# TensorE's written order in two causal attentions: at a tie the second-pass step goes ahead of the first-pass job

## The reference, cut to what matters

```python
scores = jnp.einsum('bhqd,bhkd->bhqk', q, k) * scale
scores = jnp.where(causal, scores, -jnp.inf)
attn = jax.nn.softmax(scores, axis=-1)
out = jnp.einsum('bhqk,bhkd->bhqd', attn, v)
```

## Time and profile before

| what | us |
|---|---|
| median of 3 runs (range) | 2225.05 (2218.56 to 2233.74) |
| the profiled execution, device time | 2212.26 |
| its span | 2210.4 |
| PE busy in the span | 1749.5 (79%) |
| DVE busy | 1322.6 (60%) |
| ACT busy | 915.0 (41%) |
| a2a, first job to last DVE operation | 1208.1 to 1482.2 |
| a3a, X.1 of unit 0 to last DVE operation | 1711.9 to 1952.2 |

### The profile page before, as it was taken

One profiled execution on the slowest core, in us unless ns is written; L12 is line 12 of the kernel. 1 busy time (PEld: TensorE's weight loads), 2 busy tenths in 40 slices (PEclk: granted clock), 3 DMA queues, 4 the chain that ended last, 5 costly groups with the idle time before them and its releaser, 6 DMA issues. The chain is left out here.

```text
span 2210.4 us, 33923 instructions
## 1 busy us (share of the span) xinstructions
PE 1749.5 (79%) x12419; PEld 806.9 (37%) x12439; DVE 1322.6 (60%) x2669; ACT 915.0 (41%) x1719; POOL 408.8 (18%) x335
## 2 busy tenths in 40 slices
PE   5895999737888888888475798885984998859998
PEld 3633444313333433333232343433432344333333
DVE  3224444767557766674416788805465888437888
ACT  1110222325655656565342366651222566632221
POOL 0000000166456656563003000000001000000000
PEclk8797999858999999899887799987986899979999
DMA  4100000277566666664004211000005011000000
GB/s 131 47 17 1 0 0 0 68 193 183 137 147 170 158 165 146 165 155 103 11 7 132 53 27 31 17 1 1 0 20 175 16 31 31 2 1 0 0 0 19
DMA packets 193024, 141.40 MB, mean 64 GB/s; under 512 B 55865, under 2 KB 174825, under 8 KB 192746
## 3 DMA queue, kind: packets, MB, share of 16 engines
q1 hardware_dynamic: 186250, 127.35, 22.4%
q10 hardware_dynamic: 6624, 12.06, 1.9%
HBM read 78.75 MB, written 59.90 MB: 63 GB/s over the span
## 5 line engine op out<-in xcount | busy, mean ns | idle before, releaser
L1639 DVE TENSOR_REDUCE a1a_partial<-a1a_room 128x4 f32<-128x1024 f32 x192 | 226.0, 1220 | 52.5 <-PE a1a_room L1704 52.1
L1598 ACT ACTIVATE a1a_probsT<-a1a_st 128x512 f32<-128x512 f32 (+1 forms) x416 | 204.9, 580 | 55.4 <-PE a1a_st L1737 55.1
L2061 ACT ACTIVATE a3a_probsT<-a3a_st 128x512 f32<-128x512 f32 (+2 forms) x320 | 155.2, 562 | 112.7 <-PE a3a_st L2123 70.4
L2061 ACT ACTIVATE a2a_probsT<-a2a_st 128x512 f32<-128x512 f32 (+2 forms) x320 | 155.4, 561 | 109.7 <-PE a2a_st L2123 67.2
L1978 DVE TENSOR_REDUCE a3a_maxima<-a3a_room 128x2 f32<-128x1024 f32 (+3 forms) x160 | 170.1, 1112 | 35.3 <-PE a3a_room L2094 23.0
L1978 DVE TENSOR_REDUCE a2a_maxima<-a2a_room 128x2 f32<-128x1024 f32 (+3 forms) x160 | 170.2, 1112 | 29.0 <-PE a2a_room L2094 19.7
L745 DVE TENSOR_TENSOR f_mid<-f_b,f_act 128x512 f32<-128x512 f32 x96 | 66.3, 691 | 158.9 <-ACT f_act L707 158.9
L1774 PE MATMUL a1a_ctx<-a1a_probsT,a1a_vpad 128*9 128x512 f32 (+3 forms) x1408 | 151.2, 531 | 0.8
L1503 POOL TENSOR_TENSOR a1a_shifted<-a1a_shifted,a1a_best 128x1024 f32<-128x1024 f32 x64 | 121.6, 1901 | 144.2 <-DVE a1a_best L1645 144.0
L707 ACT ACTIVATE f_act<-f_a 128x512 f32<-128x512 f32 x100 | 59.7, 597 | 203.8 <-PE f_g L678 181.2
L1704 PE MATMUL a1a_room<-stack 48*128 48x128 bf16 (+1 forms) x1376 | 112.9, 265 | 28.8 <-DVE a1a_partial L1639 14.4
(11 more groups left out here) (477 smaller groups left out, 3407.8 us busy)
## 6 DMA issues: line engine op xcount, KB each, us to landing
a1a_bands<-a_band SPq DMA_DIRECT2D x112, 192.0 KB, 3.9
a_near<-a1a_shifted SPq DMA_DIRECT2D x112, 192.0 KB, 2.9
a1a_near<-a_near SPq DMA_DIRECT2D x64, 256.0 KB, 4.1
a_band<-a1a_r_mix SPq DMA_DIRECT2D x64, 254.0 KB, 3.7
stack<-q SPq DMA_DIRECT2D x96, 96.0 KB
stack<-k SPq DMA_DIRECT2D x32, 96.0 KB
q<-a1j_parts ACTq DMA_DIRECT2D x10, 256.0 KB, 3.1
q<-a_last_parts ACTq DMA_DIRECT2D x10, 256.0 KB, 4.2
```

What stands on the lines that cost most here:

```text
L1598: nc.scalar.activation(dst, src, ACT.Exp).then_inc(exp_done, 1)
L1639: nc.vector.tensor_reduce(partial[:, g % 2, :, 1 + r].rearrange("p (a s) -> p a s", a=2), src, X_AXIS, ALU.max).then_inc(job_free, 1)
L2061: nc.scalar.activation(probsT[:, block_at % BLOCK_ROOMS, place:place + heads, lo:], src, ACT.Exp).then_inc(exp_done, 1)
```

## The change

```diff
-            if max(now, event_at) < max(now, job_at):
+            if max(now, event_at) < max(now, job_at) + 1:
                 events.pop(0)
                 order.append(event)
```

## The result

The changed kernel takes 2269.70 us (median of 4 runs, 2266.04 to 2274.09) against 2229.39 (4 runs beside it, 2218.56 to 2234.05): a ratio of **1.0189, 95% interval 1.0143 to 1.0234**. It is slower, by 1.4 to 2.3%. Forecast were 2277 us, 2236 to 2302. The profiled execution took 2266.04 us (span 2264.2) against 2212.26, 53.8 more; 52 was forecast for that difference.

A forecast was written before the change was run, and what follows sets the result against it. DVE was taken to set the period first, with TensorE nearly full too. Per attention 1.2 + 7 x 34.2 + 26.0 = 266.6 us against 240.7; 52 us more for two, put on the 2225 median: 2277 us, range 2236 to 2302.

The forecast's parts named there:

- The tail: From turn X7.1 to DVE's last operation, only half 1 of unit 7 is left: 26.0 us, a gain of 20.8.
- X0.1 later: Turn X0.1 comes 1.2 us later, because products of unit 0 now go ahead of its last jobs.
- X.1 to X.0: Five jobs with nothing beside them, then an instruction run seen before, at half clock, in every unit: 12.3 us.
- X.0 to S: From turn X.0 to first step S: 7 products with steps, and 10 jobs mostly hidden beside them: 13.4 us.
- S to X.1: From first step S to turn X.1: 12 steps, 3 products, a context and 4 jobs, paced by TensorE and ACT: 8.5 us.
- The period: One unit of the attention, sum of its three stretches: 34.2 us against 27.7 before; break-even 30.5.
- The sum: Per attention 266.6 us against 240.7, 25.9 more; 52 us more for two attentions.
- the period is set by DVE first: In the old order's unit period, DVE sets the pace, with about 24.2 us of records in 27.7.
- the pace comes from steps that wait for a bank until ACT has read it: In X.0 to S, waits for ACT's reading set the pace, 2.56 us a product, with a 0.47 us wait seen.
- The full-clock rival: Clock stays full behind X.1 because waits there are short: period 32.1 us, total 2247; chance 0.20.
- shorter tail pays: Jobs fill all waits from S to X.1, clock full: period 30.3 us, total 2222, not slower; chance 0.12.
- Deeper spells: Half clock lasts past X.0 into the next product groups: period 36.0 us, total 2302; chance 0.11.

The follow-up runs named there:

- the added reductions: One more short DVE reduction ahead of every second job, on the changed order and the old order, both with clock-keeping matmuls: 2267.01 and 2233.45 us, one run each.
- with the clock held: Changed order plus matmuls of 128 columns filling waits at lone jobs, rows and tail context turns: 2244.65 us, ratio 1.0128 to the kernel before.
- the run from unit 5: Kernel before, with ties going to the step only from second-pass unit 5 on, plus the added matmuls filling waits: 2200.68 us, ratio 0.9923.
- the first experiment: Tie rule changed in attention a2a alone, a3a keeping the order of the kernel before: 2249.78 us, one run.

## Why the prediction was right

- **The tail** was forecast at 26.0 us and is 25.8. Its terms held: 0.6 us to the rows' DMA, 2.7 for the rows (2.9 forecast), 22.5 for half 1. The last was luck in part, since the clock was at half for 6.5 us of it, as it had been before for 6.4; with the same 28 steps behind X7.1 and nothing added there, five other tails took 32.0 to 32.7 us at half clock for the most part, which the forecast did not price.
- **X0.1 later** by 1.2: from the first job to X0.1 it is 34.67 us for 33.32 in a2a and 37.54 for 36.29 in a3a, so 1.35 and 1.25.
- **X.1 to X.0**: 12.3 forecast, 12.59 measured, as one spell of half clock in every unit. The spell lasts 10.2 us (1383.4 to 1393.6) in eleven of fourteen periods, not 13; TensorE was back at full speed as X.0 came, and so the stretches after it were undisturbed.
- **X.0 to S**: 13.4, measured 13.37. **S to X.1**: 8.5, measured 8.12. The period: 34.2, measured 34.08. The terms were off by +0.29, -0.03 and -0.38, which cancel; that is luck, on a small scale.
- **The sum**: 25.9 per attention was forecast, 27.2 and 24.7 came; with 1.9 us in the rest of the program 53.8 in all. On the medians it is 40, 12 less than forecast: the forecast worked its difference out within one execution, which lay 17 us below the median of the four beside the changed kernel.
- **What was wrong is a reason, not a number.** The step "the period is set by DVE first" is not what the added reductions show, and the old order did not feed DVE "almost without a hole": from X0.1 to X7.1 it waited for TensorE for 22.7 of 193.9 us. Likewise "the pace comes from steps that wait for a bank until ACT has read it" holds for a fraction only. The stretches were priced by rows of the same or nearly the same instruction runs, and so came out right without the cause.
- **The full-clock rival** had the right price (32.1, measured 31.89) and the wrong condition: the clock was at 0.50 behind every X.1 from X0.1 to X6.1 in both attentions, 14 of 14, in the steady period behind waits of 0.99 us or less. The Trainium skill's page "TensorE: Matmul & The Clock Gate", section "Why this matters for your kernels", on which this rival drew, puts drops in mid-kernel down to idle gaps between bursts of matmuls, longer ones than these; the trace does not agree, here either. The rival by which the **shorter tail pays** needed a period under 30.5; even with the clock held it is 31.89. **Deeper spells** came in two of the fourteen periods, the first two of a2a, where the half clock reached past X.0: 35.2 and 35.7 us, close to the 36.0 of that rival. In the twelve others they did not come.

What the change does, then: a tie given to the job lets the second pass fall behind bit by bit, 59 steps of it by X7.1, and this stock is what TensorE mixes between the jobs. A tie given to the step keeps no stock. At each X.1 it is empty, so five jobs run with ACT idle, and what they leave has to be done in 21.5 us in which TensorE, as argued above, is full. Seven times 6.4 us are paid so that a tail is 21 us shorter. Not all of the 45 us is waste: the 31 steps that the tail has lost are done in the periods instead. At the 0.40 to 0.52 us that a step more cost in the run from unit 5, an estimate for them is 12 to 16 us; the half clock, 34.08 less 31.89 in a period, is 15 us, and some 13 to 17 us are left for the coarser order.

## What to carry to other kernels

When two streams share an engine, a stock of ready work of the one is what fills the waits of the other: run it down only near the end, where the stock itself becomes the tail. (Here that gained 0.8% with the clock kept by added matmuls, and nothing clear of the noise without.) Price a new order by finding its very runs of instructions somewhere in the old trace, clock included, and leave the question of which engine is the bound to an experiment. Where an engine's records are short and overlap, count them from start to start.

## What was not expected of the hardware

The half clock can last although TensorE hardly rests: in the tail at half clock its records filled 25.78 of 28 us and the clock stayed at 0.50 throughout, and in a3a of the first experiment 23.32 of 26. The same instructions in the same order ran the whole of such a tail at a mean of 0.89 in the profile of before and of 0.70 in the first experiment. Sixteen added matmuls of 128 columns ahead of each context turn, in which TensorE otherwise waits for ACT, and 32 in the wait for the rows went with tails of 25.4 to 25.8 and of 42.5 us in the six attentions of the three kernels that had only these matmuls added; without them in the tail, the short tail of 28 steps took 25.8 us four times and 32.0 to 32.7 five times. With more work on ACT one long tail still fell to half clock for the most part (56.8 us, a mean of 0.65), so they are no guarantee.
